# The first 16-head attention takes its row maximum as a channel of the key product, and clips against a bound spread by DMA

## The reference, cut to what matters

```python
# NUM_HEADS = 16, CLAMP = 10000.0, D = 16, query = _layernorm(x)
q = (query @ Wq + bq).reshape(B, Nq, H, D).transpose(0, 2, 1, 3)
k = (key_value @ Wk + bk).reshape(B, Nkv, H, D).transpose(0, 2, 1, 3)
v = (key_value @ Wv + bv).reshape(B, Nkv, H, D).transpose(0, 2, 1, 3)
attn = jnp.einsum('bhqd,bhkd->bhqk', q, k) * scale
attn = jnp.clip(attn, -CLAMP, CLAMP)
attn = jax.nn.softmax(attn, axis=-1)
x = jnp.einsum('bhqk,bhkd->bqhd', attn, v).reshape(B, Nq, Cq)
return x @ Wo + bo
```

## Time and profile before

| What | us |
|---|---|
| Median of 3 runs (5396.16 to 5409.77) | 5397.86 |
| The profiled execution, its own time | 5410.37 |
| Its span in the trace | 5408.6 |
| First 16-head attention, from the start to the end of its last y_out | 720.2 |

### The profile page before, as it was taken

How to read it: one execution, slowest core, us unless ns; L and a number is a source line. 1 busy time by engine, 2 the same in 40 slices (tenths; PEclk the granted TensorE clock), 3 DMA queues, 4 the chain that set the end, 5 groups by cost and what they waited for, 6 DMA issues and landing times. The chain is left out here.

```text
span 5408.6 us, 90306 instructions
## 1 busy us (share of the span) xinstructions
PE 4830.3 (89%) x31900; PEld 3797.7 (70%) x31900; DVE 3185.4 (59%) x9751; ACT 1848.3 (34%) x3926; POOL 1778.5 (33%) x2213
## 2 busy tenths in 40 slices
PE   6888859997778969997999699999999977999978
PEld 4555548886667858885776588888888844787845
DVE  5666658885544533316887377777777753444344
ACT  2333313333333413213555233333333323222234
POOL 2111114442214533305554033333333221555522
PEclk9999979998889989998999899999999989999989
DMA  1010011112332142213221211001100027222223
GB/s 41 29 33 29 23 40 46 53 48 61 118 102 48 50 85 70 65 48 85 69 70 55 71 31 34 29 29 31 36 29 29 25 74 237 86 94 88 78 91 108
DMA packets 320298, 333.63 MB, mean 62 GB/s; under 512 B 64805, under 2 KB 288266, under 8 KB 316778
## 3 DMA queue, kind: packets, MB, share of 16 engines
q1 hardware_dynamic: 306538, 302.60, 18.6%
q0 software_dynamic: 13312, 25.25, 2.0%
HBM read 234.72 MB, written 93.03 MB: 61 GB/s over the span
## 5 line engine op out<-in xcount | busy, mean ns | idle before, releaser
L2507 PE MATMUL fa_h<-fa_xnT,fa_w 128*128 128x256 f32 x2048 | 485.8, 383 | 0.0
L2519 PE MATMUL fa_y<-fa_w,fa_hT 128*128 128x256 f32 x2048 | 462.5, 379 | 0.0
L2507 PEld LDWEIGHTS fa_h<-fa_xnT,fa_w 128*128 128x128 f32 x2048 | 382.6, 191 | 71.2 <-issue 13.2
L2519 PEld LDWEIGHTS fa_y<-fa_w,fa_hT 128*128 128x128 f32 x2048 | 386.8, 190 | 65.0 <-issue 14.8
L2386 ACT ACTIVATE fa_hT<-fa_h,fa_b 128x256 f32<-128x256 f32 x512 | 214.5, 470 | 545.1 <-PE fa_h L2507 483.2
L994 PE MATMUL f_c_ps<-f_hs,f_diag 128*128 128x256 f32 x1536 | 355.6, 384 | 7.9 <-DVE f_hs L862 2.6
L413 DVE TENSOR_REDUCE a_mx<-a_score 128x16 f32<-128x1920 f32 x128 | 276.2, 2158 | 137.4 <-PE a_score L587 137.4
L994 PEld LDWEIGHTS f_c_ps<-f_hs,f_diag 128*128 128x128 f32 x1536 | 284.5, 190 | 58.4 <-DVE f_hs L862 21.6
L520 ACT ACTIVATE a_pT<-a_score 120x2048 f32<-120x2048 f32 x128 | 240.3, 1878 | 191.9 <-PE a_score L644 129.7
L128 POOL TENSOR_SCALAR a_rs<-a_mv 128x2 f32<-128x2 f32 x96 | 21.2, 220 | 751.8 <-DVE a_mv L122 751.7
L1533 PE MATMUL r_h<-r_xnT,r_rw 128*128 128x256 f32 x1024 | 251.3, 395 | 0.7 <-ACT r_xnT L1483 0.7
(11 more groups left out here) (452 smaller groups left out, 10911.8 us busy)
## 6 DMA issues: line engine op xcount, KB each, us to landing
cv_toep<-kernels SPq DMA_DIRECT2D x16, 2048.0 KB
x<-a_xo SPq DMA_DIRECT2D x96, 256.0 KB, 3.2
f_xb<-x SPq DMA_DIRECT2D x64, 256.0 KB, 2.8
f_xres<-x SPq DMA_DIRECT2D x64, 256.0 KB, 2.9
a_xb<-x SPq DMA_DIRECT2D x64, 256.0 KB, 3.1
e_w<-in_L_ffn_ew SPq DMA_DIRECT2D x16, 1024.0 KB, 7.0
a_cb<-in_ctx SPq DMA_DIRECT2D x96, 90.0 KB, 2.8
a_xb<-in_x SPq DMA_DIRECT2D x32, 256.0 KB, 3.4
```

The lines of the kernel that those rows point to most:

```text
L2507: last = pe.matmul(h_ps[j % 2][:, c, :], w1[:, e, k, f:f + P], xnT[it.p][:, k, :], start=k == 0, stop=k == KD - 1)
L2519: last = pe.matmul(bank[:, t * D:(t + 1) * D], hT[e % 2][:, k, t * P:(t + 1) * P], w2[:, e, k, :], start=k == 0, stop=k == KE - 1)
```

## The change

In a0 the maximum now also goes as a channel of the keys: kda and qa are built with a clip as well, `put_max` runs, and `take_off`, `nsel` and `mT` are gone. `shifted_scores(m)` gives the score less the (clipped) maximum. Clipping that difference needs 0 as the upper bound and, as the lower one, -10000 minus the query's maximum, which differs from query to query and head to head. That bound must be on all 120 key partitions. `low_out` (ScalarE, in the place of `mT_out`) makes it from `av` in the tile `low`; `keep_low` (SP) writes its 8 rows for both halves, 16 KB, to HBM (`lowest`), and after that has landed `spread_low(m)` (SP) reads them back for each half as 8 KB on each of 120 partitions, 960 KB, into `floor[m]`, of which there is one for each half. `clips(m)` takes minimum with 0 and maximum with floor in one instruction, out of `score` into `pT`, and `exps(m)` works in place in pT. So `score` is free after the clip and not after the exponential (`emptied`). `put_max` waits for `low_out`, since both read `av`. The orders of VectorE and TensorE in a0 are changed; the third attention and all other stages are not.

```diff
@@ -227,14 +227,16 @@
...
+    mxp = [[st.sb(f"mx{p}{t}", [P, KD, G, 32]) for t in range(TL)] for p in two]
+    kda = [st.sb(f"kda{p}", [P, KD, E, SK]) for p in four]
+    qa = [st.sb(f"qa{p}", [P, E, KD, S]) for p in four]
...
-        nsel = st.sb("nsel", [P, SETS, SK])
-        mxp = [[st.sb(f"mx{p}{t}", [P, G, 32]) for t in range(TL)] for p in two]
-        mT = [st.sb(f"mT{p}", [P, S]) for p in two]
-    else:
-        mxp = [[st.sb(f"mx{p}{t}", [P, KD, G, 32]) for t in range(TL)] for p in two]
-        kda = [st.sb(f"kda{p}", [P, KD, E, SK]) for p in four]
-        qa = [st.sb(f"qa{p}", [P, E, KD, S]) for p in four]
+        lowest = nc.dram_tensor(f"{name}_lowest", (B, KD, G * E, S), F32, kind="Internal").ap()
+        low = [st.sb(f"low{p}", [P, KD, S]) for p in two]
+        floor = [st.sb(f"floor{m}", [SK, G, E * S]) for m in range(KD)]
+        under = st.sb("under", [P, 1])
+        low_ready, clipped = st.sem("low_ready"), st.sem("clipped")
+        kept, floor_in = ([st.sem(f"{n}{m}") for m in two] for n in ("kept", "floor_in"))
-    KDS = 1 if clip else 2
+    KDS = 2
...
@@ -289,7 +291,21 @@
...
-            pipeline(sp, B, DEPTH, [(0, load), (6 + off, store)], **RUN)
+            def keep_low(it):
+                sp.wait_ge(low_ready, it.i + 1)
+                sp.dma_start(lowest[it.i].rearrange("m r s -> r m s"), low[it.p][0:P:DH]).then_inc(kept[it.p], 16)
+
+            def spread_low(m):
+                def step(it):
+                    if m == 0:
+                        sp.wait_ge(kept[it.p], 16 * (it.h + 1))
+                    if it.reused(1):
+                        sp.wait_ge(clipped, KD * (it.i - 1) + m + 1)
+                    sp.dma_start(floor[m][:], lowest[it.i, m].rearrange("(g e) s -> g (e s)", e=E).partition_broadcast(SK)).then_inc(floor_in[m], 16)
+                return step
+
+            spreading = [(4, keep_low), (4, spread_low(0)), (4, spread_low(1))] if clip else []
+            pipeline(sp, B, DEPTH, spreading + [(0, load), (6 + off, store)], **RUN)
...
@@ -311,8 +327,7 @@
...
-                pool.tensor_tensor(nsel[:], const["fold8"][:, 0:SETS].unsqueeze(2).to_broadcast([P, SETS, SK]),
-                                   const["minus"][:].unsqueeze(2).to_broadcast([P, SETS, SK]), ALU.mult).then_inc(made, 1)
+                pool.memset(under[:], -clip).then_inc(made, 1)
...
@@ -334,10 +349,9 @@
...
-                if not clip:
-                    pool.wait_ge(kd_ready, KDS * it.i + 1)
-                    pool.tensor_tensor(kda[it.at][:], kd[it.at][:], at_max[:].unsqueeze(1).unsqueeze(3).to_broadcast([P, KD, E, SK]),
-                                       ALU.subtract).then_inc(kd_ready, 1)
+                pool.wait_ge(kd_ready, KDS * it.i + 1)
+                pool.tensor_tensor(kda[it.at][:], kd[it.at][:], at_max[:].unsqueeze(1).unsqueeze(3).to_broadcast([P, KD, E, SK]),
+                                   ALU.subtract).then_inc(kd_ready, 1)
...
@@ -400,12 +414,8 @@
...
             def maxima(t):
                 def step(it):
-                    if clip:
-                        m = mxp[it.p][t][:, :, 0:SETS]
-                        s_in = score[:, :, 0:SETS * SK].rearrange("p g (j k) -> p g j k", k=SK)
-                    else:
-                        m = mxp[it.p][t][:].rearrange("p m g (h r) -> p m g h r", r=DH)[:, :, :, :, 0]
-                        s_in = score[:, :, 0:SETS * SK].rearrange("p g (m h k) -> p m g h k", m=KD, k=SK)
+                    m = mxp[it.p][t][:].rearrange("p m g (h r) -> p m g h r", r=DH)[:, :, :, :, 0]
+                    s_in = score[:, :, 0:SETS * SK].rearrange("p g (m h k) -> p m g h k", m=KD, k=SK)
...
@@ -413,11 +423,14 @@
...
-                        c.add(dve.tensor_scalar(m, m, clip, -clip, ALU.min, ALU.max))
+                        flat = mxp[it.p][t][:].rearrange("p m g (h r) -> p (m g h) r", r=DH)[:, :, 0]
+                        c.add(dve.tensor_scalar(flat, flat, clip, -clip, ALU.min, ALU.max))
...
             def put_max(it):
...
+                if clip:
+                    dve.wait_ge(low_ready, it.i + 1)
...
@@ -426,9 +439,11 @@
...
             def clips(m):
                 def step(it):
-                    dve.wait_ge(raw_ps, KD * it.i + m + 1)
-                    a = score[0:SK, :, :]
-                    dve.tensor_scalar(a, a, clip, -clip, ALU.min, ALU.max).then_inc(clipped, 1)
+                    dve.wait_ge(floor_in[m], 16 * (it.i + 1))
+                    if it.reused(1):
+                        dve.wait_ge(av_ps, KD * (it.i - 1) + m + 1)
+                    dve.wait_ge(st_ps, KD * it.i + m + 1)
+                    dve.scalar_tensor_tensor(pT[m][:], score[0:SK, :, :], 0.0, floor[m][:], ALU.min, ALU.max).then_inc(clipped, 1)
...
@@ -453,8 +468,8 @@
...
-                    (3, maxima(0)), (4, clips(0)), (5, reciprocals), (1, norm_stats), (3, maxima(1)), (4, clips(1)), (5, weigh),
-                    (1, norm), (5, y_out)], **RUN)
+                    (4, put_max), (3, maxima(0)), (5, reciprocals), (4, clips(0)), (1, norm_stats), (3, maxima(1)), (5, weigh),
+                    (1, norm), (4, clips(1)), (5, y_out)], **RUN)
...
@@ -478,9 +493,8 @@
...
-                    if not clip:
-                        for h in range(E):
-                            last = act.activation(qa[it.at][:, h, m, :], f, ACT.Identity, bias=qbias[:, h, m:m + 1], scale=qscale[:, h:h + 1])
+                    for h in range(E):
+                        last = act.activation(qa[it.at][:, h, m, :], f, ACT.Identity, bias=qbias[:, h, m:m + 1], scale=qscale[:, h:h + 1])
...
@@ -500,11 +514,11 @@
...
-            def mT_out(it):
+            def low_out(it):
...
-                    act.wait_ge(st_ps, 2 * it.i - 2)
-                act.copy(mT[it.p][:], av[:, 0:S]).then_inc(taken, 1)
+                    act.wait_ge(kept[it.p], 16 * it.h)
+                act.activation(low[it.p][:], by_k(av[:]), ACT.Identity, bias=under[:, 0:1], scale=-1.0).then_inc(low_ready, 1)
...
@@ -514,15 +528,19 @@
...
             def exps(m):
                 def step(it):
-                    if it.reused(1):
-                        act.wait_ge(av_ps, KD * (it.i - 1) + m + 1)
-                    act.wait_ge(st_ps, KD * it.i + m + 1)
-                    act.activation(pT[m][:], score[0:SK, :, :], ACT.Exp).then_inc(exp_ready, 1)
+                    if clip:
+                        act.wait_ge(clipped, KD * it.i + m + 1)
+                        act.activation(pT[m][:], pT[m][:], ACT.Exp).then_inc(exp_ready, 1)
+                    else:
+                        if it.reused(1):
+                            act.wait_ge(av_ps, KD * (it.i - 1) + m + 1)
+                        act.wait_ge(st_ps, KD * it.i + m + 1)
+                        act.activation(pT[m][:], score[0:SK, :, :], ACT.Exp).then_inc(exp_ready, 1)
...
-                    (4, mT_out), (2, xT_out), (5, raw_out), (4, exps(0)), (2, q_out), (2, k_out), (2, v_out), (4, exps(1))], **RUN)
+                    (4, low_out), (2, xT_out), (5, raw_out), (4, exps(0)), (2, q_out), (2, k_out), (2, v_out), (4, exps(1))], **RUN)
...
@@ -537,6 +555,8 @@
...
+            emptied = clipped if clip else exp_ready
+
@@ -578,7 +598,7 @@
...
-                        pe.wait_ge(exp_ready, 2 * it.i - 2 + t)
+                        pe.wait_ge(emptied, 2 * it.i - 2 + t)
...
@@ -596,53 +616,27 @@
...
-                    if clip:
-                        last = pe.transpose(av[:, t * P:(t + 1) * P], mxp[it.p][t][:].rearrange("p g r -> p (g r)"), const["ident"][:])
-                    else:
-                        for m in range(KD):
-                            last = pe.transpose(av[:, m * S + t * P:m * S + (t + 1) * P], mxp[it.p][t][:, m, :, :].rearrange("p g r -> p (g r)"),
-                                                const["ident"][:])
+                    for m in range(KD):
+                        last = pe.transpose(av[:, m * S + t * P:m * S + (t + 1) * P], mxp[it.p][t][:, m, :, :].rearrange("p g r -> p (g r)"),
+                                            const["ident"][:])
...
             def free_score(it, m):
...
-                    pe.wait_ge(exp_ready, KD * it.i + m)
-
-            def by_key(it, m, keys, queries, last_of):
-                for h in range(E):
-                    for g in range(G):
-                        rows = slice(g * 32, (g + 1) * 32)
-                        q = queries[rows, m, :] if clip else queries[rows, h, m, :]
-                        last = pe.matmul(score[0:SK, g, h * S:(h + 1) * S], keys[rows, m, h, :], q,
-                                         start=h == 0, stop=not clip, skip_group_check=True)
-                last.then_inc(last_of, 1)
-
-            def raw_scores(m):
-                def step(it):
-                    free_score(it, m)
-                    by_key(it, m, kd[it.at], qT[it.at], raw_ps)
-                return step
+                    pe.wait_ge(emptied, KD * it.i + m)
...
             def shifted_scores(m):
```

(21 more changed lines are left out.)

## The result

The changed kernel takes 5510.34 us (median of four runs, 5503.15 to 5517.29), the kernel before 5399.78 beside it (four runs): a ratio of 1.020 (95% interval 1.0188 to 1.0212), +110.6 us. The direction is the forecast's; the size is two and a half times it and lies outside the range.

The account below looks back on a forecast made before the run. Bound by the one-buffer score ring, 20.79 us a round; a chain across engines replaces it: 21.1 + 1.4 for the clock = 22.5, 31 rounds 697.5 + drain 20.5 = 718.0 against 674.5, +43.5 us: 5441 us, range 5385 to 5485.

Parts of the forecast that it names:

- The chain that takes the ring's place: Clip-stage round across the engines, clips(0) to next clips(0): 21.0 to 21.1 us, replacing the one-buffer score ring's 20.79.
- I take about four gaps in ten: 1.4 us a round: TensorE's clock halving behind two 2.5 us gaps a round, slowing project_v, by-key scores and attend: 1.4 us a round.
- the bound of 3.8: Most the half clock could cost a round if it always fell: 2.1 plus about 1.7 us.
- I take 5.1: Time of spread_low(0), 960 KB, on the floor's DMA path: 5.1 us, within bounds of 4.8 and 9.5.
- A spread over 6: Sign in the profile after: spread_low(0) taking over 6 us would refute its step, forecast to land in 4.9 to 5.4.
- the low clock: Main case: some low clock in the clip stage, rounds of 21.8 to 23.5 us, 5419 to 5473; chance 0.56.
- the spread lands late: Rival: 960 KB need 7.0 to 9.5 us, DMA path ends at 22.9 to 25.4, 5455 to 5532 us; chance 0.15.
- What comes before the first clip keeps its length: Start of the clip stage, maxima, turn_max and first transfers: unchanged, first clip at 45.7 us.
- The tail: Last batch's drain, last clips(0) to the end of y_out: 20.5 us, with attend(1) 3.7 at half clock.
- The clock stays up: Rival: TensorE's clock doesn't fall in the gaps, rounds of 21.1 us, +0.1 us, 5398; chance 0.22.
- Faster: Rival: low_out early enough for floor, chain doesn't close, round 17.5 us, -111.5 us, 5286; chance 0.07.

Follow-up runs that it names:

- e6_widefill: Changed kernel with floor on 128 partitions and four unread matmuls in each of TensorE's two idle gaps per round; ratio 1.0048 to the kernel before.
- e1_wide: Changed kernel with the floor spread to all 128 partitions (1024 KB for 960); ratio 1.0159 to the kernel before.
- e8_nodma: Changed kernel without keep_low and spread_low, floor a constant set once, low_out waiting for `taken`; ratio 1.0156 to the kernel before.
- e7_fill: Changed kernel, floor still on 120 partitions, with four unread matmuls in each of TensorE's two idle gaps; ratio 1.0189 to the kernel before.
- e4_source: Changed kernel with the spread reading 120 different 8 KB rows of the input instead of one row 120 times; ratio 1.0213 to the kernel before.
- e2_early: Changed kernel with low_out a slot earlier, ahead of exps(1), in ScalarE's order; ratio 0.9995 to the kernel before.
- e5_all: Changed kernel with floor on 128 partitions, q_out ahead of exps(0), low_out a slot earlier and ahead of exps(1); ratio 0.9899 to the kernel before.
- e10_clip1: Changed kernel with floor on 128 partitions, q_out ahead of exps(0), low_out ahead of exps(1), clips(1) ahead of norm; 5302.07 us, ratio 0.9818 to the kernel before.

## Why the prediction was wrong in size

**Right.** *The chain that takes the ring's place.* In the round from 314.88 the second q_out ends 6.8 us behind the clip (forecast 6.85; the q_out rows end at 321.67), clips(1) starts at 9.2 (9.10), low_out follows at 13.4 and ends at 14.0 (13.9), and the next attend starts at 15.8 (15.6). The clip is 2.29 (2.30) and put_max 1.41 (1.40). Its full-clock round is bounded by e6_widefill at 21.1 to 21.4 (21.1). keep_low took 306.05 to 307.85 = 1.8 (1.8). spread_low(1), nsel, the extra POOL product in the steady state and SP's queue showed no wait of their own. The direction came from this chain and a clock that falls in its gaps; the rows show both, so it was not luck.

The size is found by dividing the round at four starts. Means over rounds 2 to 30 in us, from the timelines:

| | e6_widefill | changed kernel | e1_wide | e8_nodma | e7_fill |
|---|---|---|---|---|---|
| clips(0) to clips(1), over project_v and by-key scores | 9.17 | 10.06 | 10.83 | 10.50 | 9.92 |
| clips(1) to attend | 6.57 | 6.57 | 6.58 | 6.59 | 6.58 |
| attend to the reciprocal | 3.72 | 4.70 | 4.57 | 4.88 | 3.72 |
| reciprocal to the next clips(0) | 1.89 | 2.95 | 1.87 | 1.68 | 3.80 |
| round | 21.35 | 24.28 | 23.86 | 23.65 | 24.02 |

The first and the third line grow with the clock, the last (1.67 at least) with the wait for the floor.

**The step that failed first: "I take about four gaps in ten: 1.4 us a round".** Where the floor is in time, e1_wide and e8_nodma, the two stretches lose 2.5 us against e6, two thirds of the bound of 3.8. In the changed kernel itself they lose 0.89 + 0.98 = 1.9. So the term was too small by 0.5 to 1.1 us a round, 15 to 34 us in 31 rounds. The text had both gaps (2.5 forecast; 2.34 and 2.98 in the rows), both victims, and the upper bound; only the weight was a guess, with two rows of 2.05 and 1.81 at hand that had both ended at half clock. Neither end was near: the full price would have been 1.3 to 1.9 too much. That it is the clock is shown: the added matmuls of e6 do nothing but keep TensorE busy, and they bring the round of e1 from 23.7 to 21.4.

**The second: "I take 5.1" for the first spread.** In the rows it took from 307.85 to the clip at 314.88, 7.0; the least of the 64 is 6.5 (their median of 10.1 holds the second of each pair, which follows the first). "A spread over 6" was named as what would refute the step, and it does. The row that was taken as nearest, e_b's one row on 128 partitions at 5.4, has the pattern of reads but not the number of partitions, and e4_source and e1_wide show that of these two the number counts. In the changed kernel the clip waits for it for 2.95 - 1.67 = 1.3 us a round, a term that the forecast put at nothing: 40 us in 31 rounds. The forecast had the low clock and the rival "the spread lands late" (7.0, a round of 22.9) as alternatives, the second with the clock up. Both came at once: 21.1 + 1.9 + 1.3 = 24.3. They are not independent either. With the spread repaired the clock's loss grows from 1.9 to 2.5, so that the spread is worth only 0.5 to 0.7 us of the round, 15 to 22 us in all; with the two gaps filled (e7) the wait grows from 1.3 to 2.1, and the late clip costs another 0.75 through the clock.

By the Trainium skill ("DMA: Bandwidth & Descriptors", section "Why a DMA increments its semaphore by 16 and not by 1"), a transfer runs on the largest number of engines up to 16 that divides the outer sizes of both sides, so by that rule on 15 for 120 partitions and 16 for 128; section "The descriptor swizzle" adds that in the case of 128 partitions each engine writes one port of SBUF. One engine fewer would be 6%, an estimate from that rule, while the rates are 213 and 389 GB/s at a like busy share. That engines then share a port might explain the rest, but no run here shows the ports or the number of engines. What is shown is the effect of the number of partitions; why stays open.

**The third: "What comes before the first clip keeps its length".** It grew by 4.4 us, in e8_nodma without the floor's transfers as well (50.2), so it is not those. The timeline shows q_out with its four more activations and kda in the first batches' path, where there is no earlier work to hide them (the first maximum starts at 33.7 instead of 30.9), the first scores at 1.98 us instead of 1.09, and norm at 2.49 beside kda instead of 1.75. These are read from the rows; no run takes them apart. The tail was 2.1 us shorter than forecast, mainly as the last attend(1) took 2.0 us where 3.7 was summed.

Together, 31 x 1.74 + 4.4 - 2.1 = 56 us over the forecast of the stage. The other stages took 7.1 less in this execution, so that it is 49 above its forecast of 5453.9; and while the execution of before stood above its median (12.5 when I forecast), this one is 7.2 below, 20 more: 69 in all, from 5441 to 5510.

**The rivals.** "The clock stays up" fell with the clock at 0.89. "Faster" (a round of 17.5) is false for this order, and true of the same arithmetic in another: its condition, low_out early enough for the floor, is what e2_early and e5_all bring about, and e10_clip1's 17.73 is that rival's round.

## What to carry to other kernels

An edit that takes work from TensorE in a chain across engines opens gaps, and what follows each gap at half clock is the bound of its price. Here half to two thirds of the bound was paid, and the length of a gap did not tell by itself which rounds paid. So take a range over most of the bound, or fill the gaps in one run and measure it. When a chain crosses the engines once a round, look first at what stands ahead of its links in each in-order queue: here three moves in two lists, with eight more partitions, turned +110.6 us into -101. A late transfer and a falling clock largely hid one another: a fix for one alone recovers little (e1 0.5 us, e7 0.2 us a round), both together 2.8. Two such rivals are to be priced together too, and not only as alternatives.

## What the hardware showed that was not expected

- The same kind of transfer to 128 partitions moved 389 GB/s and landed in 4.4 us at best, to 120 partitions 213 GB/s and 6.5 us, at a busy share of 1.01 and 0.97 of the DMA engines. The smaller transfer is the slower one.
- norm, two tensor_scalars of 256 elements in SBUF, took 0.73 us by itself and 2.18 (up to 2.49) while POOL ran tensor_tensors of 480 elements. These are rows side by side; the cause of the slowing was not tested.
- Matmuls that nobody reads made a stage faster: four in each of two gaps of about 2.5 us held the clock at 1.00 and took 2.3 us from a round of 23.7.
- How long TensorE idled did not settle the clock by itself: project_v behind the same 2.34 us ran at full clock in 14 of 24 rounds of the changed kernel and in none of 29 of e1_wide, and attend behind 0.93 us ran at half clock in 19 of 29 rounds of e5_all.
